# Batch attention of a fused two-layer kernel: another instruction order on all five engines

## The reference

```python
def _L1_ffn_ref(x, Wqkv, bqkv, Wo, bo, g1, be1, g2, be2, Wg, W1, b1, W2, b2):
    # D = 128, H = 4 heads, E = 8 experts; S = 16 is attended over, B = 512 positions
    def _mha(x, ...):
        q, k, v = jnp.split(x @ Wqkv.T + bqkv, 3, axis=-1)     # each to (B, H, S, 32)
        att = jax.nn.softmax(jnp.einsum('bhqd,bhkd->bhqk', q, k) / np.sqrt(32), axis=-1)
        o = jnp.einsum('bhqk,bhkd->bhqd', att, v)
        return o.transpose(2, 0, 1, 3).reshape(S, B, D) @ Wo.T + bo
    def _moe(x, ...):
        idx = jnp.argmax(xf @ Wg.T, axis=-1)
        for e in range(E):
            out = out + (idx == e)[:, None] * (relu(xf @ W1[e] + b1[e]) @ W2[e] + b2[e])
    y = _layer_norm(x + _mha(x, ...), g1, be1)
    return _layer_norm(y + _moe(y, ...), g2, be2)
```

## Time and profile before

| | us |
|---|---|
| median of 3 runs | 999.71 (999.56 to 1000.05) |
| the profiled execution | 999.7 |
| its span | 997.9 |
| batch attention stage within it | 638 to 828 |

### The profile page before, as it was taken

How to read it: one execution, slowest core, us unless ns; L and a number is a source line. 1 busy time by engine, 2 the same in 40 slices (tenths; PEclk the granted TensorE clock), 3 DMA queues, 4 the chain that set the end, 5 groups by cost and what they waited for, 6 DMA issues and landing times. The chain is left out here.

```text
span 997.9 us, 21606 instructions
## 1 busy us (share of the span) xinstructions
PE 838.0 (84%) x5240; PEld 616.6 (62%) x5240; DVE 825.3 (83%) x2581; ACT 605.8 (61%) x1556; POOL 707.4 (71%) x450
## 2 busy tenths in 40 slices
PE   5599999999969959999999997289887715999993
PEld 5456666666647736666666664156565505999993
DVE  5569999999958957999999998569798743999995
ACT  2656656665349945676665753377664105999992
POOL 4489999999835538999999997364997460455554
PEclk9899999999979979999999999599999556999997
DMA  9430000000000000000000000544767564544410
GB/s 252 160 88 1 1 2 1 1 1 1 1 4 1 1 1 1 12 22 16 18 22 11 22 22 22 155 118 127 205 207 210 170 202 135 142 130 134 132 57 18
DMA packets 64972, 70.54 MB, mean 71 GB/s; under 512 B 8965, under 2 KB 52178, under 8 KB 64740
## 3 DMA queue, kind: packets, MB, share of 16 engines
q1 hardware_dynamic: 50612, 47.20, 17.1%
q0 software_dynamic: 6368, 16.89, 5.0%
q10 hardware_dynamic: 7872, 5.08, 2.0%
HBM read 32.32 MB, written 24.50 MB: 57 GB/s over the span
## 5 line engine op out<-in xcount | busy, mean ns | idle before, releaser
L484 PE MATMUL a_pS<-a_kv,utri 128*128 128x360 f32 (+3 forms) x768 | 262.8, 479 | 14.9 <-POOL a_kv L474 13.6
L474 POOL TENSOR_TENSOR a_kv<-a_qk,a_vv 128x2304 f32<-128x2304 f32 (+1 forms) x64 | 253.9, 3968 | 13.8 <-DVE a_qk L445 13.5
L579 DVE TENSOR_TENSOR a_tt<-a_pS,a_qk 128x360 f32<-128x360 f32 (+3 forms) x384 | 188.6, 526 | 24.2 <-PE a_pS L484 22.6
L484 PEld LDWEIGHTS a_pS<-a_kv,utri 128*128 128x128 f32 x768 | 139.6, 192 | 96.4 <-POOL a_kv L474 23.2
L596 POOL TENSOR_TENSOR a_tt<-a_tt 128x1152 f32<-128x1152 f32 (+1 forms) x64 | 146.7, 2292 | 28.4 <-DVE a_tt L579 28.3
L2105 POOL DMA_INDIRECT out_dram<-x_o,x_place x71 | 69.4, 977 | 77.1 <-DVE x_o L2092 75.1
L607 DVE TENSOR_REDUCE a_nd<-a_tt 128x144 f32<-128x720 f32 (+3 forms) x128 | 101.5, 814 | 0.4 <-POOL a_tt L596 0.3
L1685 POOL DMA_INDIRECT ys<-m_S,m_dest x64 | 63.2, 987 | 35.1 <-issue 13.3
L544 ACT ACTIVATE a_tt<-a_pI 128x144 f32<-128x144 f32 (+1 forms) x96 | 40.1, 417 | 70.1 <-PE a_pI L496 68.4
L2043 PE MATMUL x_pZ<-w,x_hT 128*128 x568 | 76.3, 278 | 1.5 <-issue 1.4
L418 ACT ACTIVATE a_vv<-a_pQ 128x128 f32<-128x128 f32 x122 | 33.9, 278 | 66.1 <-PE a_pQ L409 65.9
(11 more groups left out here) (303 smaller groups left out, 2136.3 us busy)
## 6 DMA issues: line engine op xcount, KB each, us to landing
x_yl<-ys SPq DMA_DIRECT2D x71, 193.5 KB, 2.5
X<-xs SPq DMA_DIRECT2D x16, 256.0 KB, 5.3
kx<-m_kc SPq DMA_DIRECT2D x64, 64.0 KB
ax<-m_pc SPq DMA_DIRECT2D x64, 64.0 KB
m_S<-X SPq DMA_DIRECT2D x16, 256.0 KB, 3.1
xs<-X SPq DMA_DIRECT2D x15, 256.0 KB
w<-in_L_ffn_W_dram SPq DMA_DIRECT2D x1, 2048.0 KB
m_S<-gw ACTq DMA_DIRECT2D x6, 256.0 KB, 3.0
```

The source lines that it names most:

```text
L474: pool.tensor_tensor(kv[:, t:t + 2, :, :, :].rearrange("p t h j i -> p (t h) j i"), kk.unsqueeze(2).to_broadcast([P, 2 * H, J, D]), rows.u ...
L484: pe.matmul(pS[c][:, 0:(h1 - h0) * SC], K.utri[:, :], flat[:, h0 * SC:h1 * SC], start=True, stop=True).then_inc(u_done, 1)
L579: v.tensor_tensor(tt[:, t, h0:h1, :, 0:D], pS[c][:, 0:(h1 - h0) * SC].rearrange("p (h j i) -> p h j i", i=D, j=J), q[:, h0:h1, :].unsqueez ...
```

## The change

Only `attend_and_route` is touched. No arithmetic changes.

- VectorE: `vec_choose` and `vec_dest` are split into single operations, which stand between the softmax and statistics operations of the step. `link` (signal and wait at once) becomes `done` (signal) and, ahead of the operation that needs it, `last` (wait).
- The scan's constant is copied to `ramp`, in the PSUM bank pS, once per round, and the scan reads it there. The wait of the reciprocal for the scan before it goes.
- GpSimd, steps up to 11: xb, scale, four scatters, h, where passes and scatters alternated. Steps from 12 on stay.
- ScalarE: exp moves ahead of the evictions of q and k, the place numbers up, and at the end of the step ScalarE's queue issues bands 2 and 3 of ax, which wait for pc; the standard deviations of a round (act_rstd) come behind that.
- SyncE's queue: residual copy, bands 0 and 1 of ax, then kx; before kx, residual copy, all of ax.
- TensorE: v ahead of q and k.
- A function `vec_xb` is added and not called.

```diff
@@ vec_reciprocal
-            wait(v, hot_ready, (g - 2) // 2)
@@ sp_ax -> ax_bands
-        def sp_ax(sp, g):
+        def ax_bands(q, g, bands):
-            for c in range(4):
+            for c in bands:
...
+        def vec_choose_carry(v, r):
+            v.wait_ge(sm_ready, min(2 * r + 5, G))
+            v.tensor_copy(ramp, reset[:, :, :].rearrange("p e n -> p (e n)")).then_inc(ramp_done, 1)
...
+        def vec_choose_equal(v, done, last, r):
+            n = tiles(r)
+            last()
+            done(v.tensor_tensor(lg[:, 0:n, :], lg[:, 0:n, :], by_e(best[:, 0:n], n), ALU.is_ge))
...
+        def vec_choose_scan(v, last, r):
+            last()
+            v.wait_ge(ramp_done, r + 1)
+            v.tensor_tensor_scan(upto[:, :, :].rearrange("p e n -> p (e n)"), ramp,
                                  hot[:, :, :].rearrange("p e n -> p (e n)"), 0.0, ALU.mult, ALU.add).then_inc(hot_ready, 1)
@@ pe_step
             if there(s + 2):
+                pe_v(pe, s + 2)
                 pe_qk(pe, s + 2)
-                pe_v(pe, s + 2)
@@ act_step
+            if there(s):
+                act_exp(act, s)
             if there(s + 2):
                 act_q(act, s + 2)
                 act_k(act, s + 2)
-            if there(s):
-                act_exp(act, s)
...
+            if there(s):
+                ax_bands(act, s, (2, 3))
+            if even(s - 3) and s < G - 1:
+                act_rstd(act, (s - 3) // 2)
@@ pool_step
-            if there(s - 5):
-                pool_row(pool, s - 5, 0)
+            if there(s + 3):
+                pool_xb(pool, s + 3)
             if there(s + 4):
                 pool_scale(pool, s + 4)
             if there(s - 5):
+                pool_row(pool, s - 5, 0)
                 pool_row(pool, s - 5, 1)
+                pool_row(pool, s - 5, 2)
+                pool_row(pool, s - 5, 3)
             if there(s + 4):
                 pool_h(pool, s + 4)
...
@@ sp_step
-                    if there(s + 2):
-                        sp_kx(sp, s + 2)
                     if there(s - 2):
                         sp_xb(sp, s - 2)
                     if there(s):
-                        sp_ax(sp, s)
+                        ax_bands(sp, s, (0, 1))
+                    if there(s + 2):
+                        sp_kx(sp, s + 2)
```

More of the change, by code:

```diff
@@ L1635, in vec_choose, with vec_choose_offset @@
[L1635 to L1641, removed]
-                                 hot[:, :, :].rearrange("p e n -> p (e n)"), 0.0, ALU.mult, ALU.add).then_inc(hot_ready, 1)
+        def vec_choose_offset(v, done, last, r):
+            n = tiles(r)
+            last()
+            done(v.tensor_tensor(lg[:, 0:n, :], lg[:, 0:n, :], c8[:, :].unsqueeze(1).to_broadcast([P, n, E]), ALU.add))
@@ new lines, in vec_choose_best, with vec_choose_ties @@
+        def vec_choose_best(v, done, last, r):
+            n = tiles(r)
+            last()
+            done(v.tensor_reduce(best[:, 0:n], lg[:, 0:n, :], AX.X, ALU.max))
+        def vec_choose_equal(v, done, last, r):
+            n = tiles(r)
+            last()
+            done(v.tensor_tensor(lg[:, 0:n, :], lg[:, 0:n, :], by_e(best[:, 0:n], n), ALU.is_ge))
+        def vec_choose_ties(v, done, last, r):
+            n = tiles(r)
+            last()
+            done(v.tensor_tensor(lg[:, 0:n, :], lg[:, 0:n, :], tie[:, :].unsqueeze(1).to_broadcast([P, n, E]), ALU.mult))
@@ new lines, in vec_choose_first, with vec_choose_hot @@
+        def vec_choose_first(v, done, last, r):
+            n = tiles(r)
+            last()
+            done(v.tensor_reduce(first[:, 0:n], lg[:, 0:n, :], AX.X, ALU.max))
+        def vec_choose_hot(v, done, last, r):
+            n = tiles(r)
+            last()
+            wait(v, pos_ps, r)
+            if r == G // 2 - 1:
+                done(v.memset(hot[:, :, 5:9], 0.0))
+            done(v.tensor_tensor(hot[:, :, 1:1 + n].rearrange("p e n -> p n e"), tie[:, :].unsqueeze(1).to_broadcast([P, n, E]),
+                                 by_e(first[:, 0:n], n), ALU.is_equal))
@@ L1750, in x_stats, with vec_step @@
                     tile_stats(v, K, K.X, n, stats)
-        def vec_step(v, s, link):
+        def vec_step(v, s, done, last):
+            choice = (s - 4) // 2 if even(s - 4) and s < G else None
+            place = (s - 5) // 2 if even(s - 5) and s < G else None
             if there(s - 2):
@@ L1756, in vec_step @@
                 vec_logits(v, s - 2)
-                vec_stats(v, s - 2)
-            if even(s - 5) and s < G:
-                vec_dest(v, link, (s - 5) // 2)
+            if place is not None:
+                vec_dest_pick(v, place)
+                vec_dest_sum(v, done, place)
+            if there(s - 2):
+                vec_stats(v, s - 2, (0,))
+                vec_stats(v, s - 2, (1,))
             if there(s):
                 vec_max(v, s)
+            if there(s - 2):
+                vec_stats(v, s - 2, (2,))
+            if there(s):
                 vec_shift(v, s)
+            if place is not None:
+                vec_dest_cast(v, last, place)
             if there(s - 2):
-                vec_var(v, s - 2)
+                vec_stats(v, s - 2, (3,))
+            if place is not None:
+                vec_dest_carry(v, done, place)
+            if choice is not None:
+                vec_choose_carry(v, choice)
+                vec_choose_logits(v, done, last, choice)
+            if there(s - 2):
+                vec_var(v, s - 2, (0, 1))
+                vec_var(v, s - 2, (2, 3))
             x_stats(v, s)
@@ L1875, in _, with done, last, link @@
                 count = [0]
-                def link(ins):
+                def done(ins):
                     count[0] += 1
                     ins.then_inc(chain, 1)
-                    v.wait_ge(chain, count[0])
+                def last():
+                    wait(v, chain, count[0])
+                def link(ins):
+                    done(ins)
+                    last()
                 v.tensor_tensor(gb[:, :], K.rows[:, 3, :], K.tab[:, 2, :], ALU.mult).then_inc(gate_done, 1)
@@ L1897, in after_step @@
                     v.memset(pad[:, TO:TO + 1], float(B * T)).then_inc(pads_ready, 1)
-                run(v, lambda v, s: vec_step(v, s, link),
+                run(v, lambda v, s: vec_step(v, s, done, last),
                     before={0: set_tables, 12: lambda: after_step(12)})
```

105 lines of the change are left out of this document (69 added, 36 removed).

## The result

**The changed kernel takes 1002.94 us (median of 7 runs, 1001.71 to 1005.84) beside 999.25 for the kernel before (7 runs): ratio 1.0038, 95% interval 1.0021 to 1.0056.** It was forecast at 992.8. It is 3.7 us slower, where 6.9 us less were expected.

The account below looks back on a forecast made before the run. GpSimd's 64th scatter was to end the stage. Group 14's output matmul would end 6.9 us sooner (2.5 before h(15)'s transposes, 2.4 to values(12), 0.8 in step 14, 1.2 in ax(14)): 999.7 to 992.8 us, range 988.5 to 999.8.

Parts of the forecast that it names:

- What bounds the stage: Batch attention stage: ends when GpSimd has issued its 64th scatter; 27.4 us after group 14's output matmul stay untouched.
- From T(15) to out(14): Drain, from TensorE's transposes of h(15) to the end of group 14's output matmul: 4.4 us less.
- From T(15) to values(12): Drain, from TensorE's transposes of h(15) to its value matmuls of group 12: 6.9 us, 0.4 saved by VectorE's earlier probabilities.
- Values(12) to pc(14): Drain, from group 12's value matmuls to group 14's transposed probabilities: only VectorE's step shortens, by 0.8 us.
- broken links: VectorE, step with a choice: eight dependent small operations parted from what needs them, 0.10 us saved each, 0.8 together.
- From pc(14) to the end of out(14): Drain, group 14's transposed probabilities to its output matmul's end: two queues issue the band copies, 1.2 us sooner.
- So they close up on GpSimd about step 9: Middle of the stage: TensorE and VectorE catch up with GpSimd, so h(15)'s transposes start at 758.0 instead of 760.54.
- the logits operation ... may wait where GpSimd's three passes now stand in a row: VectorE's choice: logits, with two SBUF inputs, may contend with GpSimd's passes; no size was given in the sum.
- first scatter 698.85: GpSimd's start in the stage: first scatter at 698.85, after two issues, xn, scale and a gap; before, 698.27.
- pc(4): Start of the stage: group 4's transposed probabilities done at about 694.5 instead of 695.19.
- rival B: GpSimd falls further behind because xn(9) comes later, and the drain gets no shorter: 998.5 us, chance 0.10.
- Rival A: ScalarE cannot carry the band copies, so xn and exp come late every step: +11 us, 1004, chance 0.12.

Follow-up runs that it names:

- dve_back: The changed kernel with VectorE's old order put back, the ramp staying in PSUM: 1000.18 us, ratio 1.0011 to the kernel before.
- rstd_psum: The changed kernel plus a VectorE copy of the rstd values into PSUM, where logits and mean read them: 1000.57 us, ratio 1.0022 to the kernel before.

## Why the prediction was wrong, point by point

- **What bounds the stage: right.** Out(14), 20 scatters without a wait and 9 us of block end came out nearly unchanged (27.4 and 8.5).
- **From T(15) to out(14): right in size by luck, not in its parts.** -4.5 came, -4.4 was forecast. From T(15) to values(12): 7.2 instead of 9.3, near the forecast's 6.9. Values(12) to pc(14): 10.4 instead of 12.7, -2.3 for the -0.8 of the broken links; here the granted clock was 1.00 where the kernel before had 0.69. dve_back, with the links as before, took 11.3 at 1.00, so the links may be worth about the 0.8 and the clock the rest; that is one execution of each, and no run parts the two. From pc(14) to the end of out(14): 9.1 instead of 9.2, where -1.2 was forecast: ScalarE's two issues took 2.46 us at 788.84 instead of 1.25, and SyncE's two the same 2.46 beside them, so two queues ended hardly sooner than the 2.83 of one in the kernel before.
- **"So they close up on GpSimd about step 9", T(15) at 758.0: wrong by 10.0 us.** Forecast 119.3 after gb, measured 129.3: the first scatter 5.4 too late, GpSimd's way from there to the end of h(15) 61.0 instead of 59.2, and 2.8 between h(15) and T(15), which stood in TensorE's queue behind values that waited for ax.
- **The step that failed is the holds, "the logits operation ... may wait where GpSimd's three passes now stand in a row", which was seen and carried at nothing.** The sum gives it no price; the only reason beside it, that steps 9 to 12 are held by GpSimd, is given for the scan. It does not cover the holds: the cast that is held makes dest, for which GpSimd itself waits (0.84 in an odd step). How much of the rest goes by way of rank, scores and xn, which stand behind the held operations, was not followed row by row. Priced from the earlier trace rows, where one pass held the scan for 1.75 more, three passes at 1.29 would have been up to 3.9 per choice. Measured: 7.1 us for all holds (1.0038 to 0.9967).
- **The cast was not in the sum at all, because half a rule was quoted.** In these traces casts and copies with one SBUF input were held up to 3.91 us (a cast in rstd_psum). The trace of the kernel before had it too, on a small scale: its cast took 0.17 at 697.13, where no pass ran, and 0.55 at 714.04, amid the pass xb. The Trainium skill's "SBUF — State Buffer", section "Who interferes with whom", names copy and cast among the instructions that can, under conditions on their operands, contend with GpSimd, and says that a reduction on trn2 never does; the prediction gave the limit of one SBUF input without that exception. The trace agrees with the whole rule: 3.03 for the copy, 0.15 for the reduction in its place.
- **The start, "first scatter 698.85", was wrong by 5.4.** pc(4), put at 694.5, ended at 59.2 after gb instead of 55.8; ahead of it the first two operations of step 3's variance took 0.99 and 1.31 on VectorE (0.67 and 0.18 before), and the granted clock fell to 0.66 for some 10 us after TensorE had waited 2.13 for probabilities. From pc(4) on it took 6.3 instead of 4.35: 0.8 until ScalarE, still at hT and the weights, issued, and 1.0 at the end for dest. That 0.8 is the first condition of rival B (ScalarE still busy with hT and the weights when pc comes), which has no place in the sum. Undoing the stop gives 5.0 us back at the first scatter and about 4.2 of the whole.
- **Rival A was the right side with a smaller part.** Its 1004 us is near the measured 1002.9, its mechanism (a stop for pc in ScalarE's queue, xn late) is real, and costs 4.2 us; it was priced at 11 and needed no holds. That its number came near is luck.
- **The pieces.** Holds 7.1, h 1.7 (not told from nothing) and the stop 4.3 lead one after the other from 1.0038 to 0.9907, so they add up to these 13.1 us by construction. What checks them is the stop: 4.2 alone in the changed kernel, 4.3 as the last of the three. On GpSimd's old order it was 1.9 (0.9974 to 0.9955), so the prices hold beside each other's orders only. With the three mended the kernel is 8.9 us faster than before, so edits of this kind can carry a gain of the forecast's size.

## What to carry to other kernels

Before putting GpSimd's passes in a row, list what the other engine will run beside them: two SBUF inputs, or a copy or cast from SBUF to SBUF, waited here for the end of the whole row, whatever its size. The cure was one operand or the result in PSUM, or a reduction in place of a copy; another place in the order helped only where no passes stood. A DMA issued from a computing engine's queue belongs behind the work that others wait for, since its wait for its source stops everything queued after it.

## What the runs showed of the hardware

- A held operation does not get in between two passes that follow each other: the cast waited from 718.66 to 722.49, over three passes of 1.3 us, and ended with the third. Eight elements cost as much as sixty-four.
- The hold goes on to the next operation of the kind when the first is taken away (logits 2.81, then cast 3.83, then copy 3.03), so that mending one of three gained 1.6 us, two 3.1 and all 7.1 (the first two within the intervals).
- Copies from SBUF to PSUM (0.22 amid the passes) and casts from PSUM to SBUF (0.17) were not held in any row read here.
- Short matmuls of no use in TensorE's waits kept the granted clock at 1.00 where it was 0.65, with no time gained that the runs can tell.
